# A transformer block on one core: the order of work in the last tile

## The reference

```python
h = layernorm(x)
q, k, v = (h @ wq.T + bq), (h @ wk.T + bk), (h @ wv.T + bv)   # 32 heads of 32
scores = einsum('bshd,bstd->bsht', q, k) / sqrt(32)   # heads of one row among each other
x1 = x + einsum('bsht,bstd->bshd', softmax(scores), v)

h2 = layernorm(x1)
logits = h2 @ gate_w.T                                # 8 experts, the best 2 are used
w_full = one-hot of the best two * softmax of their logits
low = einsum('bsd,erd->ebsr', h2, lora_A)             # 8 experts of rank 16: 128 numbers a row
out = x1 + h2 @ base_w.T + base_b + 2 * einsum('ebsr,eor,bse->bso', low, lora_B, w_full)
```

## Time and profile before

| | us |
|---|---|
| median of three runs | 1345.84 |
| lowest, highest | 1344.07, 1347.09 |
| the profiled execution, its own time | 1345.48 |
| its span, first to last instruction | 1343.3 |

### The profile page before, as it was taken

The page is one execution under the profiler, slowest core; times in us unless marked ns, Lnnn a source line. Parts: engine busy times, 40 slices in busy tenths (PEclk is TensorE's granted clock), DMA queues, the critical chain, the costliest instruction groups (busy, mean ns, idle before and its releaser), DMA issues.

```text
span 1343.3 us, 29100 instructions
## 1 busy us (share of the span) xinstructions
PE 1238.6 (92%) x11920; PEld 622.0 (46%) x11920; DVE 1143.1 (85%) x1533; ACT 669.8 (50%) x982; POOL 262.7 (20%) x246
## 2 busy tenths in 40 slices
PE   0677899999999999999999999999999999999994
PEld 0253444554444445544444455444444454444442
DVE  5658889888898898888988988889889888898883
ACT  8964455444544554445445544454455444544540
POOL 0020222211112222111122222121222221212220
PEclk9898999999999999999999999999999999999997
DMA  9631333333223333332233333322333333223221
GB/s 350 246 94 42 85 78 78 94 94 92 62 76 82 78 78 94 94 93 62 76 82 78 78 94 94 93 61 75 82 78 78 94 94 94 62 75 82 63 55 40
DMA packets 167667, 120.91 MB, mean 90 GB/s; under 512 B 141408, under 2 KB 142432, under 8 KB 167648
## 3 DMA queue, kind: packets, MB, share of 16 engines
q1 hardware_dynamic: 167648, 120.66, 33.1%
HBM read 53.51 MB, written 16.78 MB: 52 GB/s over the span
## 4 chain that ended last, share of the span: by engine, by line
issue 60%; POOL 14%; ACT 10%; DMA 7%; DVE 4%; PE 3%; POOLq 0%; DVEq 0%; ACTq 0%
DMA x_hi<-row_hi 7%; POOL work L500 5%; POOL work L488 4%; ACT work L616 3%; ACT row_hi L612 3%; ACT row_hi L599 2%; DVE work L772 2%; POOL columns L483 1%; POOL columns L476 1%; PE dense_acc L1093 1%; PE acc L1033 1%; PE acc L1042 1%; ACT row_hi L618 0%; ACT columns L614 0%; ACT w_hi_k L567 0%
## 5 line engine op out<-in xcount | busy, mean ns | idle before, releaser
L1093 PE MATMUL dense_acc<-base_parts,x_hi 128*128 128x512 f16 x1024 | 305.8, 380 | 0.0
L325 ACT COPY work<-work 32x512 f16<-32x512 f16 x384 | 235.9, 614 | 9.9 <-POOL work L494 1.2
L1093 PE MATMUL dense_acc<-base_parts,x_lo 128*128 128x512 f16 x512 | 194.5, 380 | 0.0
L599 ACT CAST row_hi<-work 128x1024 f16<-128x1024 f32 x32 | 33.5, 1046 | 286.7 <-DVE work L772 286.7
L1033 PE MATMUL acc<-w_hi_k,x_hi 128*128 128x512 f16 x512 | 124.5, 387 | 48.0 <-DVE w_lo_k L733 34.7
L806 DVE SCALAR_TENSOR_TENSOR work<-acc,acc_to_a,biases_sb 128x512 f32<-128x512 f32 x192 | 143.5, 748 | 21.8 <-PE acc L1042 15.7
L1093 PEld LDWEIGHTS dense_acc<-base_parts,x_hi 128*128 128x128 f16 x1024 | 99.6, 100 | 110.0 <-issue 1.0
L1033 PE MATMUL acc<-w_hi_q,x_hi 128*128 128x512 f16 x512 | 123.9, 386 | 12.1 <-DVE work L806 9.3
L1033 PE MATMUL acc<-v_parts,x_hi 128*128 128x512 f16 x512 | 121.0, 379 | 0.7 <-DVE work L806 0.7
L1042 PE MATMUL acc<-w_hi_q,x_lo 128*128 128x512 f16 x512 | 121.5, 380 | 0.0
L1042 PE MATMUL acc<-w_hi_k,x_lo 128*128 128x512 f16 x512 | 121.2, 380 | 0.0
(11 more groups left out here) (145 smaller groups left out, 2042.8 us busy)
## 6 DMA issues: line engine op xcount, KB each, us to landing
work<-x_dram SPq DMA_DIRECT2D x64, 512.0 KB, 3.3
work<-work SPq DMA_DIRECT2D x256, 64.0 KB, 2.0
out_dram<-work SPq DMA_DIRECT2D x32, 512.0 KB, 2.7
work<-wT_dram SPq DMA_DIRECT2D x19, 512.0 KB, 10.8
v_parts<-wT_dram SPq DMA_DIRECT2D x8, 512.0 KB, 6.8
base_parts<-wT_dram SPq DMA_DIRECT2D x5, 512.0 KB, 15.9
biases_sb<-bias_dram SPq DMA_DIRECT2D x4, 512.0 KB, 11.5
x_hi<-row_hi SPq DMA_TRANSPOSE x64, 3.1
```

What stands on the lines that cost most here:

```text
L325: copy(diag[c * QD:(c + 1) * QD, :, c, j::NQ, :], src).then_inc(vdiag_ready, 1)
L599: nc.scalar.copy(row_hi[:, :], xn).then_inc(row2_hi, 1)
L1093: nc.tensor.matmul(dense_acc[n][:, :], rows_part[:, k, :], w_part[:, k, cols], start=(k == 0 and m == 0), stop=False)
```

## The change

It touches the last step and the tail; steps 0 to T-2 stay as they are.

- The residual of tile T-1 gets a buffer of its own, `x1_last`, which is `soft`, the buffer of the probabilities. So writing it no longer waits until `finish` has read the `x1` of tile T-2, but waits for the transpose of the probabilities (`pt_ready`).
- In the last step DVE does `gate_rest` of tile T-2 behind the low part of the probabilities, where `finish` stood. ACT does `low_copy` of T-2 behind its last spread copies.
- In the last step PE does both halves of the base product of T-2 without the low-rank part (`dense_halves`). In the tail, `turn_low` and `dense_lora` of T-2 follow the context of T-1.
- In the tail, PE then does the 32 matmuls with high rows of T-1's base product, then its experts, then the 16 with low rows, then `turn_low` and `dense_lora`.
- DVE does `finish` of T-2 in the tail, behind `row_lo` of T-1.
- SP stores tile T-1 in two halves of the columns, each behind its own `finish`.

```diff
+        x1_last = soft
@@ sync, behind the steps
             turn2_hi(T - 1)
             turn2_lo(T - 1)
-            sp.wait_ge(base_free, 2 * T + 2)
-            sp.dma_start(rows(out, T - 1), y).then_inc(y_stored, 16)
-            sp.wait_ge(y_stored, 16 * (T + 1))
+            for n in range(NB):
+                s = slice(n * HALF, (n + 1) * HALF)
+                sp.wait_ge(base_free, 2 * T + 1 + n)
+                sp.dma_start(rows(out, T - 1)[:, s], y[:, s]).then_inc(y_stored, 16)
+            sp.wait_ge(y_stored, 16 * (T + 2))
@@ gpsimd, tail
-                base_bias(t - 1)
+                base_bias(t - 1, x1_last)
@@ scalar, step
-                if prev:
+                if prev and nxt:
                     low_copy(t - 1)
...
                 for c in C_ACT_LAST:
                     spread_v(nc.scalar.copy, c)
+                if prev and not nxt:
+                    low_copy(t - 1)
@@ vector, attention_end
-                dve.wait_ge(base_free, 2 * p + 2)
+                if x1 is not x1_last:
+                    dve.wait_ge(base_free, 2 * p + 2)
@@ vector, step
-                if prev:
+                if prev and nxt:
                     gate_rest(t - 1)
-                else:
+                elif not prev:
                     flag_low_parts()
...
-                if prev:
-                    finish(t - 1, 0)
-                    finish(t - 1, 1)
+                if prev and not nxt:
+                    gate_rest(t - 1)
+                elif prev:
+                    finish(t - 1, 0, x1)
+                    finish(t - 1, 1, x1)
@@ vector, tail
-                attention_end(t - 1)
-                norm2(t - 1, t)
+                dve.wait_ge(pt_ready, t)
+                attention_end(t - 1, x1_last)
+                norm2(t - 1, t, x1_last)
                 dve.wait_ge(row2_hi, t)
                 nc.vector.tensor_tensor(row_lo[:, :], xn, row_hi[:, :], ALU.subtract).then_inc(row2_lo, 1)
+                finish(t - 2, 0, x1)
+                finish(t - 2, 1, x1)
                 gate_top(t - 1)
                 gate_rest(t - 1)
-                finish(t - 1, 0)
-                finish(t - 1, 1)
+                finish(t - 1, 0, x1_last)
+                finish(t - 1, 1, x1_last)
@@ tensor
+            def dense_halves(p):
+                pe.wait_ge(base_free, 2 * p + 1)
+                dense(0, 0, KC)
+                pe.wait_ge(base_free, 2 * p + 2)
+                dense(1, 0, KC)
+
+            def dense_terms(n, first, last, start):
+                cols = slice(n * HALF, (n + 1) * HALF)
+                for m, (rows_part, w_part) in enumerate(parts_of[first:last]):
+                    for k in range(KC):
+                        nc.tensor.matmul(dense_acc[n][:, :], rows_part[:, k, :], w_part[:, k, cols],
+                                         start=(start and k == 0 and m == 0), stop=False)
@@ tensor, step
-                    dense_all(t - 1)
+                    if nxt:
+                        dense_all(t - 1)
+                    else:
+                        dense_halves(t - 1)
@@ tensor, tail
                 context(t - 1)
+                turn_low(t - 2)
+                dense_lora(t - 2)
+                pe.wait_ge(x2hi_ready, 16 * t)
+                for n in range(NB):
+                    pe.wait_ge(base_free, 2 * t - 1 + n)
+                    dense_terms(n, 0, 2, True)
                 experts(t - 1)
-                dense_all(t - 1)
+                for n in range(NB):
+                    dense_terms(n, 2, 3, False)
+                turn_low(t - 1)
+                dense_lora(t - 1)
```

More of the change, by code:

```diff
@@ L495, in v_low, with base_bias @@
                                         ALU.subtract).then_inc(v_lo_ready, 1)
-            def base_bias(p):
+            def base_bias(p, x1):
                 pool.wait_ge(xn2_ready, p + 1)
@@ L524, in step @@
                 if prev:
-                    base_bias(t - 1)
+                    base_bias(t - 1, x1)
                 else:
@@ L863, in gate_rest, with finish @@
                     op0=ALU.mult, op1=ALU.mult).then_inc(low_ready, 1)
-            def finish(p, n):
+            def finish(p, n, x1):
                 s = slice(n * HALF, (n + 1) * HALF)
@@ L873, in finish, with attention_end @@
                                                in1=x1[:, s], op0=ALU.mult, op1=ALU.add).then_inc(base_free, 1)
-            def attention_end(p):
+            def attention_end(p, x1):
                 dve.wait_ge(ctx_acc, p + 1)
@@ L888, in attention_end, with norm2 @@
                 ln_stats(p, 1, x1, mean_ready2, var_ready2)
-            def norm2(p, rows_before):
+            def norm2(p, rows_before, x1):
                 dve.wait_ge(row1_lo, rows_before)
@@ L928, in step @@
                     add_bias(t, 0, FIRST, 0, a_acc, a_biased)
-                    attention_end(t - 1)
+                    attention_end(t - 1, x1)
                     add_bias(t, 1, FIRST, 1, a_acc, a_biased)
-                    norm2(t - 1, t + 1)
+                    norm2(t - 1, t + 1, x1)
                     turn_first(t)
```

## The result

| | before | after |
|---|---|---|
| median of 20 runs, us | 1345.74 | 1347.49 |
| lowest to highest | 1344.07 to 1347.38 | 1346.28 to 1348.46 |
| profiled execution, own time; span | 1345.48; 1343.3 | 1347.96; 1345.9 |

The ratio after to before is 1.0013, with a 95% interval of 1.0007 to 1.0019: slower by 1.75 us, 0.13%. In a later batch the change measured 1346.45 against 1344.97, ratio 1.0010 (1.0001 to 1.0019).

What follows compares the result with a forecast made beforehand. Matmuls bound the run (PE 92% busy), but the tail's last waits decide: PE starts at 1323.9, + 14.6 to the low-rank part, `finish` to 1341.17, store to 1343.9, +0.6 us. Median 1346.4; 8 in 10: 1343.8 to 1349.3.

Steps and rivals of the forecast that it cites:

- the direction that was likeliest: Whole kernel: the time stays the same within 0.2% (2.7 us), chance 0.78; faster 0.08, slower 0.14.
- the landing: Tail, SP: high transpose right behind the store of T-2 takes 3.75 us to land, against 3.08 alone.
- the slow clock: Tail, PE: half clock for 4.5 us after PE's start, 2.25 us lost; ends 3.9 and 5.04 us.
- the start of `finish`: Tail, DVE: the last `finish` starts 1.16 us after the low-rank part starts and takes 1.51 us.
- the end: Tail: bare turn and copy 0.65 us; half-size last store saves 0.6 us of 3.37; span ends at 1343.9.
- Last step: Last step: moving the gate behind the probabilities starts the context 1.57 us earlier, at 1306.56; bounds 0 and 1.57.
- 2.46 us for the gate: Last step, DVE: the gate rows take at most 2.46 us at their new place and cost nothing.
- SP: Tail: the store of T-2 waits for `finish` and holds the high transpose until 1320.03 instead of 1315.80.
- 13 in 2.70 us: Tail, PE: 13 matmuls took 2.70 us, so 16 low-row matmuls take 3.3 us and hide the gate.
- A: Tail: the store doesn't hold the transposes, all comes 4.9 us earlier, median 1341.5; chance 0.05.
- B: Tail, PE: clock low over all 32 high-row matmuls, 6.7 us lost, +4.4, median 1350.8; chance 0.06.
- C: Tail: the transpose begins only when the store has landed, +1.6 us, 1348.0; chance 0.11.

Runs made afterwards that it cites:

- e6: The kernel of e1 with the gate of tile T-2 back in front of the sum of the exponentials: 1343.43 us, 0.9988 of before.
- e1: The changed kernel with both transposes of tile T-1 issued on SP ahead of the wait for `finish` of T-2 and its store: 1341.10 us, again 1341.36.
- e2: The changed kernel with SP's wait for `finish` of T-2 still ahead of the transposes, but the store behind them: 1345.67 us, 1.0003 of before.
- e9: The kernel of e8 with 30 more extra matmuls between the last step's base product and the last context: 1340.66 us, 0.9969 of before.
- e5: The kernel of e1 with PE's tail in the old order, experts first, then the whole base product: 1342.40 us, 0.9984 of before.
- e10: The kernel before with 210 extra matmuls in the tail's pause on PE: 1343.17 us, 0.9983 of before.
- e7: The kernel of e1 with 140 extra matmuls in the tail's pause on PE: 1341.13 us, 0.9972 of before.
- e8: The kernel of e1 with 100 extra matmuls in the tail's pause on PE: 1341.09 us, 0.9965 of before.
- e4: The changed kernel with the last store whole instead of in halves: 1347.60 us, 1.0017 of before.

## Why the prediction held, point by point

The time came out at 1347.49, inside the range; the direction that was likeliest, the same within 0.2%, is what was measured, and the ratio's interval lies on the slow side of 1. The forecast of +0.6 us was 1.15 us too low (0.9 in the later batch): a third of what was measured. In the tail no errors cancelled: the landing, the slow clock, the start of `finish` and the end were all put too low, and the range was wide enough for their sum.

- **Last step.** Forecast -1.57 us for the context; measured -1.64 against the scores of the same profile. e6 confirms that the gate's move does it. That the sum doesn't wait for POOL's addition was right: 1.22 us beside it. What the prediction didn't see is that a row of the gate is slow beside it: 2.01 us for one column, against 0.16. Its 2.46 us for the gate came from the tail, where POOL is idle, and happened to fit the new place for the same reason. An estimate from the rows of before: without these 1.85 us the transpose of the probabilities would end at 1302.59, and ACT is busy until 1303.17 (1302.90 + 0.27 of `low_copy`), so all but 0.3 us of the gain was to be had with the gate where it was. No run tests that.
- **SP.** Right in place and cause: high transpose forecast at 1320.03, or 1320.68 with the 0.65 us by which this profile's scores start later; measured 1320.67. e1 and e2 show that it was the queue's order: 5.6 to 5.9 us in all, of which the wait is 4.6. What the prediction took for given, that `row_lo` takes 2.39 us, goes with another addition of POOL beside it (1316.35 to 1318.69 before): in the first half of a step the same operation (line 899) takes 1.22. `finish`, and with it the store, waits behind it.
- **The landing behind the store.** Mis-sized: 3.75 us taken, 4.50 measured. The upper bound was 1.6 more than what I took. The load of the earlier trace rows was issued 1.1 us ahead, the store here 0.4. The trace agrees with the rule of the Trainium skill, "DMA: Bandwidth & Descriptors", "Queues, rings and completion order", in that the isolated row (3.08) is not the answer: the transpose landed 0.96 us behind the store. In all four profiles with the store ahead an instruction fetch ran in the same transfer too; e2 had such a fetch and no store and landed after 3.2, so the fetch alone was not it. Whether the two together made the extra 0.65 to 0.85 us (4.40 to 4.60 in these four against 3.75) is open.
- **The slow clock.** Mis-sized in this profile: 4.5 us taken, 5.4 seen, 0.43 us more lost. It isn't a constant: the 32 high-row matmuls take 7.07 us at the upper level (e9), 9.71 in the change's profile (2.6 lost), 9.41 in e1's (2.3 lost) and 8.42 in the second profile of the change (1.35 lost). After a pause of 7 to 14 us the slow stretch behind PE's start lasted from 2.7 us (e5) to 5.7 (e2), and the prediction had taken 3.9 and 5.04 for the ends. So one value for it was too little; it needed a range of its own from 1.3 to 2.8 us lost. e10 measures the whole term at 2.1 us on the median of before, against 2.52 in one profile.
- **The end.** The turn and copy stand bare for 0.63 us (0.65 taken); `finish` starts 1.27 us behind the low-rank part instead of 1.16; from its end to the span's end are 2.86 us (2.77 taken). The "13 in 2.70 us" of the prediction counts the turn of `low` among the matmuls: the 16 low-row matmuls took 3.45 us and not 3.3, and the gate stayed hidden under them.
- **The sum.** 0.75 + 0.43 + 0.11 + 0.09 = 1.38 us over the forecast within the tail (landing, clock, start of `finish`, end), and 0.65 from the unchanged part of the profiled execution: 0.6 + 1.38 + 0.65 = 2.63 against 1345.9 - 1343.3 = 2.6. The 0.65 is a difference of two executions and not of the kernels; the medians differ by 1.75.
- **The rivals.** A, the change as it seems to be meant, is e1: forecast 1341.5, measured 1341.1 and 1341.4. B (the clock low over all 32 matmuls) did not happen. Nor did C, though the landing stood halfway between my value and its price: a transpose that begins when the store has landed (1324.20) would by C's own sum land 3.08 us later, not 0.96.

## What to carry to other kernels

When a step is moved later on one engine, look up every queue on which something waits for it, and read what stands behind that wait: a store that was harmless at 1308 held two transposes at 1320, and moving two lines on SP was worth 5.6 to 5.9 us where the whole change had cost 1.5 to 1.75. When a tiny row takes microseconds, look for what runs beside it on another engine. Price a pause of TensorE with the slow matmuls that follow it (2.1 us in e10). Filling it helped the kernel before; on e1 no gain was measured (e7, e8, e9), and a rest of 2.8 us lost the clock again in one profile of two. The simplest version that beats both kernels is e1, at 0.9970 of before.

## What the runs showed that I had not expected

- A 16 KB instruction fetch takes one of the 16 DMA engines for 0.9 us, and a transpose that is due to land 0.5 us after its begin then gets its last part 1.5 to 1.6 us late. In e7's profile that took 1.6 of the 2.3 us that the clock gave back. With 40 matmuls less (e8) it began at 1322.93 and not at 1319.94, behind the landing.
- SP's issue of the high transpose takes longer directly behind the store: 1.96 to 2.53 us in the four profiles, against 1.25 alone. In these four a fetch began during the issue or just before it; with such a fetch and no store it was 1.83 (e2). So the low transpose is late too.
- In the profiles of e1 again, e5, e6 and e7 the clock fell during the last context, 0.4 to 1.1 us after its start and behind a pause of 2.1 to 3.7 us, and its 96 matmuls took 1.83 to 2.41 us instead of 1.52. In those of the change, e1 to e4 and e8 it did not, with pauses of 1.9 to 2.2 us, nor in e9, which fills the pause. A pause of 2 us costs sometimes nothing and sometimes 0.9 us on the path.
